# Delta rule of a fused layer stack: loops begin at step 8, five TensorE waits and one row block rearranged

## The reference, cut to what matters

```python
attn = jnp.where(strict_lower, -(k_beta @ jnp.swapaxes(k, -1, -2)), 0.0)
for i in range(1, chunk):
    row = attn[..., i, :]
    new = attn[..., i, :i] + jnp.einsum('...j,...jk->...k', row, attn[..., :, :i])
    attn = attn.at[..., i, :i].set(new)
attn = attn + eye                    # the inverse of a unit lower triangle
u, w = attn @ v, attn @ k_beta
def step(S, inp):                    # scanned over the chunks
    u_adj = u_i - w_i @ S
    o_i = q_i @ S + where(lower_incl, q_i @ k_i.T, 0) @ u_adj
    return S + k_i.T @ u_adj, o_i
```

## Time and profile before

| | us |
|---|---|
| median of 3 runs | 1314.3 (1311.65 to 1316.34) |
| profiled execution, its own time | 1315.79 |
| its span, first to last instruction | 1314.1 |
| PE busy | 1183.2 (90%) |
| DVE busy | 773.8 (59%) |
| TensorE clock granted, mean | 0.940 of 2.4 GHz |
| stretch of `delta_rule`'s PE work | 858.5 to about 1152 |

### The profile page before, as it was taken

The page is one execution under the profiler, slowest core; times in us unless marked ns, Lnnn a source line. Parts: engine busy times, 40 slices in busy tenths (PEclk is TensorE's granted clock), DMA queues, the critical chain, the costliest instruction groups (busy, mean ns, idle before and its releaser), DMA issues. The chain is left out here.

```text
span 1314.1 us, 35807 instructions
## 1 busy us (share of the span) xinstructions
PE 1183.2 (90%) x12725; PEld 879.9 (67%) x12726; DVE 773.8 (59%) x1828; ACT 477.3 (36%) x1157; POOL 490.3 (37%) x709
## 2 busy tenths in 40 slices
PE   6999999989999999992899898668888999789998
PEld 5888888867777777771445444347777889656665
DVE  5778888844322222222888899747754666534553
ACT  1111111123222222220688888613343444323332
POOL 4333666631541111105577764423343455300000
PEclk9999999989999999996899999768798999969999
DMA  9999920011331111112245653663463344300001
GB/s 309 374 349 383 384 86 33 34 37 53 121 112 65 64 63 59 62 56 66 59 125 141 182 156 98 157 174 89 83 132 95 106 117 117 96 0 29 28 29 44
DMA packets 220106, 156.61 MB, mean 119 GB/s; under 512 B 111888, under 2 KB 201488, under 8 KB 219984
## 3 DMA queue, kind: packets, MB, share of 16 engines
q1 hardware_dynamic: 210672, 129.51, 33.4%
q0 software_dynamic: 9312, 25.44, 5.7%
HBM read 64.47 MB, written 90.44 MB: 118 GB/s over the span
## 5 line engine op out<-in xcount | busy, mean ns | idle before, releaser
L945 PE MATMUL ps_sc<-w,a_qeo 128*128 x568 | 183.3, 466 | 0.0
L945 PEld LDWEIGHTS ps_sc<-w,a_qeo 128*128 128x128 f32 x568 | 104.0, 193 | 46.4 <-issue 2.5
L753 DVE TENSOR_TENSOR a_stm<-a_vpad,ps_sc 128x352 f32<-128x352 f32 x71 | 37.0, 521 | 163.4 <-ACT a_vpad L517 161.0
L423 POOL DMA_DIRECT2D x_slots<-a_stm x66 | 36.3, 550 | 218.8 <-issue 218.8
L1506 DVE SCALAR_TENSOR_TENSOR d_cout<-cin,d_taps,d_cout 128x512 f32<-128x512 f32 x144 | 101.7, 744 | 15.1 <-ACT d_cout L1382 15.0
L1690 PE MATMUL d_pp<-d_xT,d_w_p 128*128 128x512 f32 x192 | 101.6, 660 | 6.2 <-ACT d_xT L1364 6.2
L913 PE MATMUL ps_kv<-w,a_stm 128*128 x426 | 103.7, 379 | 1.2 <-DVE a_stm L746 1.2
L913 PEld LDWEIGHTS ps_kv<-w,a_stm 128*128 128x128 f32 x426 | 80.9, 190 | 24.2 <-issue 2.5
L2512 PE MATMUL g_pp<-g_xT,g_w_g 128*128 128x512 f32 x192 | 90.6, 610 | 0.7 <-ACT g_xT L2364 0.7
L517 ACT ACTIVATE a_vpad<-ps_sc 128x352 f32<-128x352 f32 x71 | 32.9, 463 | 158.2 <-PE ps_sc L945 140.2
L2147 PE MATMUL u_bank_g<-cin 64*64 64x256 f32 x256 | 68.5, 442 | 10.2 <-DVE u_S L2038 5.9
(11 more groups left out here) (281 smaller groups left out, 2734.5 us busy)
## 6 DMA issues: line engine op xcount, KB each, us to landing
x_slots<-a_zeros SPq DMA_DIRECT2D x32, 1024.0 KB, 10.6
rec<-kve SPq DMA_DIRECT2D x32, 384.0 KB, 3.0
cin<-rec SPq DMA_DIRECT2D x32, 384.0 KB, 3.7
a_qeo<-x_slots SPq DMA_DIRECT2D x71, 128.0 KB
x_slots<-a_stm POOLq DMA_DIRECT2D x66, 128.0 KB
rec<-d_act_out SPq DMA_DIRECT2D x32, 256.0 KB
cin<-rec SPq DMA_DIRECT2D x32, 256.0 KB, 3.3
w<-in_w SPq DMA_DIRECT2D x4, 1408.0 KB, 14.2
```

The lines of the kernel that those rows point to most:

```text
L945: mm = pe.matmul(ps, e_xT[:, q, k, :], w13[:, s, k, bass.ds(e_hidden, 1), :], start=(k == 0), stop=(k == KD - 1))
```

## The change

- `PART` becomes `[0, 3, 5, NG]`: the late inverses are two parts, groups 3 and 4, and groups 5 to 7. Rows of the first stand in steps 2 to 8, rows of the second in steps 9 to 16. Group 3 is sent in step 9, group 4 in step 10, and groups 5, 6, 7 in steps 17, 18, 19. SP waits for the first part's sends at step 12 and for the second part's at step 20. The semaphores `sub_own`, `t_sent` and `l_back` are divided to match.
- In DVE's step the rows stand between L2081 (`ss`) and L2084 (the subtraction for the high rows).
- `singly` is dropped for PE, ACT and POOL: their loop begins at step 8 (`DEPTH` 5, rounded up to a multiple of 4). DVE has `singly=17` (loop from step 20), SP 21 (loop from step 24).
- PE gets ten products of the identity with itself, 128x128 each, behind its first two waits, into a bank that is not in use yet.
- PE's five waits named above are left out; `x32_out` and `y_out` remain in those steps in which A or M is absent, `stm_done` where G is absent.

```diff
-PART = [0, 3, NG]
-ROWS_AT = {2: (1, 7), 3: (7, 10), 4: (10, 12), 5: (12, 13), 6: (13, 14), 7: (14, 15), 8: (15, 16)}
-SEND_AT = {9: (3, 4), 10: (5, 6), 11: (7,)}
+PART = [0, 3, 5, NG]
+ROWS_AT = {2: (1, 1, 5), 3: (1, 5, 8), 4: (1, 8, 10), 5: (1, 10, 12), 6: (1, 12, 14), 7: (1, 14, 15), 8: (1, 15, 16),
+           9: (2, 1, 5), 10: (2, 5, 8), 11: (2, 8, 10), 12: (2, 10, 12), 13: (2, 12, 13), 14: (2, 13, 14), 15: (2, 14, 15), 16: (2, 15, 16)}
+SEND_AT = {9: (1, (3,)), 10: (1, (4,)), 17: (2, (5,)), 18: (2, (6,)), 19: (2, (7,))}
...
                 if isinstance(t, int) and t == GROUP * PART[1]:
-                    sp.wait_ge(t_sent[1], 16 * SENDS * (NG - PART[1]))
+                    sp.wait_ge(t_sent[1], 16 * SENDS * (PART[2] - PART[1]))
+                if isinstance(t, int) and t == GROUP * PART[2]:
+                    sp.wait_ge(t_sent[3], 16 * SENDS * (NG - PART[2]))
...
                 if isinstance(t, int) and t in SEND_AT:
-                    if t == min(SEND_AT):
-                        sp.wait_ge(sub_done, 1)
-                    for u in SEND_AT[t]:
+                    n, groups = SEND_AT[t]
+                    sp.wait_ge(sub_done, n)
+                    for u in groups:
                         for s in range(2):
-                            send_inverses(sp, t_out, t_mat, u, s, t_sent[1])
-            pipelined(sp, NT, DEPTH, step, unroll=4, singly=GROUP * PART[1] + 1)
+                            send_inverses(sp, t_out, t_mat, u, s, t_sent[2 * n - 1])
+            pipelined(sp, NT, DEPTH, step, unroll=4, singly=GROUP * PART[2] + 1)
...
-            pipelined(pool, NT, DEPTH, step, unroll=4, singly=GROUP * PART[1] + 1)
+            pipelined(pool, NT, DEPTH, step, unroll=4)
...
-            pipelined(act, NT, DEPTH, step, unroll=4, singly=GROUP * PART[1] + 1)
+            pipelined(act, NT, DEPTH, step, unroll=4)
...
                     dve.tensor_reduce(ss[:, :], heads(sq[:, :]), AX.X, ALU.add).then_inc(ss_done, 1)
+                if isinstance(i, int) and i in ROWS_AT:
+                    n, lo, hi = ROWS_AT[i]
+                    if lo == 1:
+                        dve.wait_ge(l_back[n], 16 * 2 * (PART[n + 1] - PART[n]))
+                    inverse_rows(dve, t_out, l_in, prod, sub_own[n - 1], n, lo, hi)
+                    if hi == SUB:
+                        dve.wait_ge(sub_own[n - 1], 2 * (SUB - 1))
+                        dve.tensor_copy(...).then_inc(sub_done, 1)
                 if B:
                     dve.wait_ge(rest_of_ks, b + 1)
...
-                if isinstance(i, int) and i in ROWS_AT:
...
-            pipelined(dve, NT, DEPTH, step, unroll=4, singly=GROUP * PART[1] + 1)
+            pipelined(dve, NT, DEPTH, step, unroll=4, singly=max(ROWS_AT) + 1)
...
             pe.wait_ge(g_zeroed, 1)
+            for n in range(10):
+                pe.matmul(b_o[:, 0:P], ident[:, :], ident[:, :], start=True, stop=True)
...
                     wait(pe, s_out, b)
-                    wait(pe, less2_done, b)
...
                     wait_apart(pe, zeroed, x32_out, a)
-                    wait_apart(pe, zeroed, p2_out, a - 1)
...
                 if M:
-                    wait_apart(pe, zeroed, x32_out, m + 1)
+                    if not A:
+                        pe.wait_ge(x32_out, m + 1)
...
                     pe.wait_ge(o3_done, c + 1)
-                    wait(pe, y_out, i - 4)
+                    if not M:
+                        wait(pe, y_out, i - 4)
...
-                    pe.wait_ge(stm_done, b + 1)
+                    if not G:
+                        pe.wait_ge(stm_done, b + 1)
...
-            pipelined(pe, NT, DEPTH, step, unroll=4, singly=GROUP * PART[1] + 1)
+            pipelined(pe, NT, DEPTH, step, unroll=4)
```

More of the change, by code:

```diff
@@ L1269, in _ @@
                 sp.wait_ge(l_sent, 16 * GROUP * (u + 1))
-                load_l(sp, l_mat, l_in, u, l_back[0 if u < PART[1] else 1])
+                load_l(sp, l_mat, l_in, u, l_back[sum(u >= first for first in PART[1:])])
             send_qk(NG - 1, (NG - 1) % 2)
@@ L1843, in heads @@
             return ap.rearrange("p (h c) -> p h c", h=H)
-        sub_own = sem("sub_own")
+        sub_own = [sem(f"sub_own{n}") for n in range(2)]
         sub_done = sem("sub_done")
@@ L1913, in step @@
                     sp.wait_ge(l_sent, 16 * GROUP * NG)
-                    load_l(sp, l_mat, l_in, NG - 1, l_back[1])
+                    load_l(sp, l_mat, l_in, NG - 1, l_back[2])
                 if isinstance(t, int) and t == 3:
@@ L2081, in step @@
                     dve.tensor_reduce(ss[:, :], heads(sq[:, :]), AX.X, ALU.add).then_inc(ss_done, 1)
+                if isinstance(i, int) and i in ROWS_AT:
[5 more added lines that the diff above has]
+                        dve.wait_ge(sub_own[n - 1], 2 * (SUB - 1))
+                        dve.tensor_copy(t_out[:, PART[n]:PART[n + 1], :, 1, :],
+                                        t_out[:, PART[n]:PART[n + 1], :, 0, :].rearrange("p g i c -> p g c i")).then_inc(sub_done, 1)
                 if B:
@@ L2598, in build @@
         got = ctx.enter_context(nc.sbuf_tensor("got", [P, 2, GROUP, 2, D], F32))
-        t_sent = [ctx.enter_context(nc.semaphore(f"t_sent{n}")) for n in range(3)]
+        t_sent = [ctx.enter_context(nc.semaphore(f"t_sent{n}")) for n in range(4)]
         l_in = ctx.enter_context(nc.sbuf_tensor("l_in", [P, NG, SUB, SUB], F32))
         small = ctx.enter_context(nc.sbuf_tensor("small", [P, NT, 5 * NH1], F32))
-        l_back = [ctx.enter_context(nc.semaphore(f"l_back{n}")) for n in range(2)]
+        l_back = [ctx.enter_context(nc.semaphore(f"l_back{n}")) for n in range(3)]
         cin = ctx.enter_context(nc.sbuf_tensor("cin", [P, 2, 6, HIST + GW], F32))
```

## The result

The changed kernel took 1284.69 us (median of 4 runs, 1281.51 to 1286.93). The kernel before, run beside it on the same chip, took 1314.94 (1311.65 to 1316.34). The ratio is 0.9772, 95% interval 0.9743 to 0.98.

The account below looks back on a forecast made before the run. PE, working 90% of the span, was held by idle and low-clock time. Gains of 14.5 (steps 3 to 9), 9.8 (12 to 19) and 0.9 (waits), less 3.5, 0.8 and 2.6, made 18.3 us: 1296.0 us, range 1283 to 1307.

Parts of the forecast that it names:

- Late code, then a loop that stays in place: PE's issue stalls, 10.03 us in steps 11 to 19, are late code; a loop from step 8 stays in seven packets.
- Steps 3 to 9: Stretch forecast at 65.3 us against 79.8: floor 49.4, rows 3.2, stalls 1.1 and low clock 0.7 a step.
- Rows, 3.2 us: In steps 3 to 9, late rows exceeding the 1.55 us hidden on VectorE would delay PE by 3.2 us.
- rival C: Late code in steps 3 to 11 costs next to nothing, fetches catching up beneath VectorE's rows: 1280 us, chance 14%.
- Low clock, 0.7 a step: PE's lowered clock beside late-code stalls would cost 0.7 us in each of steps 3 to 11; ends none and double.
- Steps 10, 11 and 12 to 19: Steps 10 and 11 forecast at 18.9 us against 15.4, loss 3.5; steps 12 to 19 at 62.8 against 72.6, gain 9.8.
- the room of 1.55 us: Ahead of the high subtraction, 1.55 us of late rows per step are hidden from PE; only the excess costs.
- Steps 20 to 32: Looped stretch forecast to change little: 0.9 us gained by leaving out PE's five waits, 0.8 lost to sends.
- Sends, 0.8 lost at step 21: Step 20 waits for group 7's send, so SP runs late and tile 20 delays step 21; 0.8 us lost.
- Rival A: The loop needs eight packets and doesn't stay; each of five repeats fetches again, 8.5 us a turn: 1338 us, chance 10%.
- Rival D: The high subtraction is as tight as the low one, so rows aren't hidden: 21.7 us more, 1318 us, chance 5%.
- Rival B: Late code in steps 3 to 11 costs half more, 1.8 us in nine steps: 8 us more, 1304 us, chance 13%.

Follow-up runs that it names:

- fourth experiment: The changed kernel with the loops of PE, ACT and POOL beginning at step 16 again; 1302.24 us, ratio 0.9894 to the kernel before.
- first experiment: The changed kernel without the ten identity products, all else as changed; 1367.99 us, ratio 1.0392 to the kernel before.
- seventh: The changed kernel without late inverses: their rows and copies left out, a tiny memset releasing the sends; 1277.01 us, ratio 0.9712.
- ninth experiments: The changed kernel with rows earlier, thicker in steps 2 to 11, copies in steps 7 and 15, products ahead of PE's first two waits; 1275.87 us.
- second experiment: The changed kernel with the ten products moving 8 columns instead of 128, the same 40 instructions; 1283.21 us, ratio 0.9755.

## Why the prediction was right, and where its sizes failed

**Late code, then a loop that stays in place.** Right in mechanism and in size. The loop begins about 31 instructions behind a boundary (the boundary in step 8 lies 107 pairs into it); the forecast was 18, give or take 15. By the same count it ends near 1635, in its seventh packet, and q8 is silent through all repeats. The stalls of steps 8, 9 and 11 lie 249 and 371 pairs apart, two and three packets. The one packet that the earlier trace rows have while the loop of before repeats starts at 1127.8, behind the loop's exit at 1123.06; from 1045 to 1123 there is none. The Trainium skill, "Runtime: NRT & Kernel Launch", section on instruction fetch mechanics, advises to unroll, because of a window of two pages. The measurements decide against that for this kernel: unrolling steps 12 to 15 again costs 17.5 us (fourth experiment). Of the 2048 instructions that the same section names, eight packets, a loop could use seven here: the one that touches eight fetched nine in a turn (first experiment).

**Steps 3 to 9: gain 19.9 against 14.5.** This is the step of the sum that failed most, and two terms in it. "Rows, 3.2 us": they cost nothing that shows there, where the code is late in the same steps. The prediction had this as the lower bound ("0, if stalls of the code cover them") and as rival C, and added up two costs that hide each other. The waits ahead of the high subtraction's reader, for which it named about 1 us in steps 6, 8 and 12 and 2 in step 16, were 0.29, none, 0.43 and 1.62. "Low clock, 0.7 a step": what is left of the stretch after floor, stalls and the one wait is 59.85 - 49.4 - 6.1 - 0.3 = 4.1 us for rows and low clock together (and 0.76 of it is step 3's wait for `u_stm`), where 3.2 + 4.9 = 8.1 stood in the sum. That sharing-out rests on one profile. The 1.1 us of stalls a step were near: 6.1 us in seven steps are 0.87.

**Steps 10, 11 and 12 to 19.** 18.4 and 63.0 us against 18.9 and 62.8. The rows' durations (within 0.1 us; only the copy of two groups was off, 0.59 us against 0.92), the room of 1.55 us and the long step 16 were right, and the seventh and ninth experiments confirm it.

**Steps 20 to 32: gain 3.8 against 0.1.** Three terms. The waits were right: 0.08 us a step. "Sends, 0.8 lost at step 21" did not happen: SP waited 1.1 us for them, PE not at all. And the exit's stall of 2.72 us, a row that the prediction used only to place the eighth boundary, was never asked about: it went. It is a term of the sum that was left at nothing, worth 2.9 us in steps 32 and 33 by the first profile of the kernel before and 5.7 by the second. By the count, the boundary at 2048 now falls to the start of the short step 33. The stall stands in all kernels whose loop begins at step 16 (2.72, 2.72, 2.71 and 2.29 us) and in the one with the five waits (1.29), and in none of the other nine. That the code's position decides it was only argued, and one kernel speaks against so simple a rule: without the products the count puts that boundary into the middle of step 32, and nothing stalls there.

**Rival A** had the mechanism and 8.5 us a turn right. Its 1338 was too low for what it described: the kernel without the products took 1368. The term that failed is the low clock, which rival A left out altogether. **Rival D** is out: no wait for the high subtraction as long as the rows. **Rival B** is out, with 8.66 us of stalls in nine steps. **Rival C** was half right, as said.

**The products.** 4.48 us against 4.5. The forecast gave them 1.9 us of clock back at the start. The second experiment and the first show about 3 there, so that less than the forecast's 2.6 is theirs: with them it took 14.2 to 14.8 us, with none or with small ones 13.3. The kernel before took 12.2 and 12.3, at a clock of 0.64 instead of 0.50; what that clock came from is not shown.

**Still open:** what makes the start of the stage wander between 847 and 857 us; how much of the division in two is gain (1.7 us by the medians, with an uncertainty of some 6); whether the large products pay; and no run varied the loop's start in small steps, so how close to the edge of the seventh packet it may end was not tried.

## What to carry to other kernels

Work out, from the stalls' distances and the instruction queue's packets, where a loop's code lies before moving its start: one packet more than fits costs every turn, and the low clock behind the stalls can double it, while a few instructions ahead of the loop can save it. Don't add up costs that hide each other: where PE stands for late code, another engine's extra work beneath it can be free, and removing one of two such causes alone can show nearly nothing. A stall that a row shows at the end of a loop belongs in the sum as much as those in its middle, for an edit ahead of it can move it or take it away.

## What was unexpected of the hardware

- Ten 128x128 float32 products took 4.48 us with 128 columns and 4.44 with 8: the columns were all but free. With 32x32 weights and 32 columns they took 1.24.
- Five fulfilled waits, 51 ns each in the profile, cost 0.08 us per looped step, not 0.26.
- A loop that touches eight packets of code fetched nine in a turn; one that touches seven fetched none.
- Stalls of 0.4 to 3.0 us five times in a turn of four steps brought the granted clock down to 0.78 and 0.80, and that cost nearly as much as the stalls: 38 and 43.5 us.
- In the kernels before and after, late code showed only where PE had little else to wait for. At 11.4 us a step, with 16.1 us of waits for VectorE, the boundaries of steps 3 to 9 passed without a stall of their own (before); at 8.7 us a step (steps 3 to 11 after) they gave 0.67 to 2.56 us, and not at every boundary: six stalls on some 14.
